# A decoder kernel: its input in three transfers, another form of the Fourier attention's output projection, and ScalarE's lift between its sines

## What is computed

```
scores = einsum('bhqd,bhkd->bhqk', Q, K) / sqrt(D_K) + rel_bias_matrix
x = layernorm(x + softmax(scores) @ V @ Wo.T + bo)
```

```
p  = einsum('blhd,dm->blhm', q or k, proj_mat) / sqrt(D_HEAD)       # m = 128
q', k' = concat([cos(p), sin(p)], -1) / sqrt(D_KMAP)
kv  = einsum('blhm,blhd->bhmd', k', v)
out = einsum('blhm,bhmd->blhd', q', kv).reshape(B, L, 128)
x   = layernorm(x + out @ Wo.T + bo)
```

## Time and profile before

| | |
|---|---|
| median of 3 runs | 1683.41 us (1680.90 to 1689.48) |
| profiled execution, own time | 1688.41 us |
| its span (first to last instruction) | 1686.6 us |
| TensorE busy | 1455.5 us, 86% |
| VectorE busy | 1106.4 us, 66% |
| ScalarE busy | 916.2 us, 54% |
| GpSimd busy | 310.8 us, 18% |
| mean granted clock of TensorE | 0.953 of full speed |
| Fourier phase | from 548.8 to 996.5 us of the span |

### The profile page before, as it was taken

The page is one execution under the profiler, slowest core; times in us unless marked ns, Lnnn a source line. Parts: engine busy times, 40 slices in busy tenths (PEclk is TensorE's granted clock), DMA queues, the critical chain, the costliest instruction groups (busy, mean ns, idle before and its releaser), DMA issues. The chain is left out here.

```text
span 1686.6 us, 31393 instructions
## 1 busy us (share of the span) xinstructions
PE 1455.5 (86%) x12291; PEld 894.3 (53%) x12306; DVE 1106.4 (66%) x2343; ACT 916.2 (54%) x1255; POOL 310.8 (18%) x285
## 2 busy tenths in 40 slices
PE   5999869999798687888888847999999999999972
PEld 3666637777565333433334324566666666666542
DVE  2666646665332598898988952445567667776778
ACT  1332224444454588988888854445565565665433
POOL 2334234443000211101110012111111211210001
PEclk9999979999799799999999986999999999999995
DMA  4000000000000100000000000322222222222220
GB/s 160 2 2 2 2 20 14 12 11 2 1 1 1 51 1 1 1 1 1 1 1 1 1 10 7 71 62 63 68 59 57 69 69 60 60 66 63 57 53 16
DMA packets 39825, 50.73 MB, mean 30 GB/s; under 512 B 9216, under 2 KB 21632, under 8 KB 39296
## 3 DMA queue, kind: packets, MB, share of 16 engines
q1 hardware_dynamic: 39392, 48.06, 11.1%
q10 hardware_dynamic: 288, 0.67, 0.1%
HBM read 13.04 MB, written 2.10 MB: 9 GB/s over the span
## 5 line engine op out<-in xcount | busy, mean ns | idle before, releaser
L1521 DVE TENSOR_TENSOR l_px<-psum,l_share 128x1024 f32<-128x1024 f32 x64 | 78.4, 1225 | 155.5 <-PE psum L1240 101.8
L1381 ACT ACTIVATE l_prob<-psum,l_bias 128x1024 f32<-128x1024 f32 x64 | 71.3, 1114 | 173.6 <-PE psum L1220 173.6
L1229 PE MATMUL psum<-l_XT,l_A 128*128 128x256 f32 x512 | 132.4, 404 | 8.7 <-ACT l_th L1389 6.1
L1215 PE MATMUL psum<-l_th,l_XT 128*128 128x512 f32 x256 | 125.5, 613 | 0.9 <-DVE stream L1528 0.5
L1275 PE MATMUL psum<-l_px,l_N 128*128 128x256 f32 x512 | 124.6, 387 | 1.0 <-ACT l_r L1421 1.0
L1240 PE MATMUL psum<-l_prob,l_X 128*128 128x512 f32 x256 | 123.1, 603 | 0.0
L1229 PEld LDWEIGHTS psum<-l_XT,l_A 128*128 128x128 f32 x512 | 96.9, 200 | 23.0 <-ACT l_th L1389 8.1
L1502 DVE TENSOR_REDUCE l_top<-psum 128x8 bf16<-128x1024 f32 x64 | 78.1, 1221 | 44.8 <-PE psum L1290 44.8
L1275 PEld LDWEIGHTS psum<-l_px,l_N 128*128 128x128 f32 x512 | 94.7, 193 | 18.4 <-issue 4.7
L791 PE MATMUL psum<-f_projX,f_kT 64*128 64x512 f32 x256 | 72.7, 646 | 35.2 <-DVE f_frac L1050 19.2
L793 PE MATMUL psum<-f_qT,f_projX 64*128 64x512 f32 x256 | 72.3, 640 | 32.6 <-DVE f_frac L1050 24.7
(11 more groups left out here) (281 smaller groups left out, 3262.4 us busy)
## 6 DMA issues: line engine op xcount, KB each, us to landing
l_share<-l_recip SPq DMA_DIRECT2D x512, 64.0 KB, 2.0
early_weights<-in_weights SPq DMA_DIRECT2D x1, 2405.0 KB, 15.6
c_cs<-in_ctx SPq DMA_DIRECT2D x16, 128.0 KB, 2.1
f_qf<-in_l_mats SPq DMA_DIRECT2D x1, 2048.0 KB, 7.4
l_craw<-in_ctx SPq DMA_DIRECT2D x16, 128.0 KB, 2.2
out<-l_normed SPq DMA_DIRECT2D x16, 128.0 KB, 2.0
late_weights<-in_weights SPq DMA_DIRECT2D x1, 1089.0 KB, 11.0
relbias<-in_relbias ACTq DMA_DIRECT2D x1, 512.0 KB, 4.6
```

The costliest lines, as they stand in the source:

```text
L1215: nc.tensor.matmul(ps[:, SC + n, :], XT[:, q % 3, k, :, :], th[:, q % 2, k, 8 * n:8 * n + 8, :], start=True, stop=False)
L1229: last = nc.tensor.matmul(ps[:, RO + j // 2, (j % 2) * 256:(j % 2 + 1) * 256], A[:, QB * k + j, :], XT[:, q % 3, :, 1, :], start=True, sto ...
L1381: nc.scalar.activation(prob[:, b % 4, :, :], ps[:, SC:SC + 2, :], ACT.Exp, bias=bias[:, b:b + 1]).then_inc(s["exped"], 1)
L1521: nc.vector.tensor_tensor(px[:, q % 2, :, k, :], ps[:, GA:GA + 2, :].rearrange("p a (h s) -> p (a h) s", s=S), share[:, (b // 2) % 2, b % ...
```

## The change

There are four edits. The input comes in three transfers: 4 tiles, 8 tiles, and the other 20, the last of them with the rest of the weights issued in the first phase (`load_rest`); the bias has a semaphore of its own, and TensorE doesn't wait for VectorE's memsets. At the start of the Fourier phase, VectorE norms the first group and GpSimd does `projX` after that; the waits for `consts` stand later on TensorE and ScalarE. The output projection takes 64 tokens of the kept outputs as stationary operand and the weights as moving one, so that its result has tokens on partitions: copy and transposes are gone, and the residual comes at n = 4 from bank 6. ScalarE's lift stands between sine and cosine of the unit two before.

The diff, cut to its core:

```
@@ attention_phase @@
+        if not cross:
+            @block.sync
+            def _(sp):
+                c["load_rest"](sp)
...
                 if cross:
                     pe.wait_ge(s["staged"], d + 1)
+                elif 2 * d >= FIRST_TILES:
+                    pe.wait_ge(c["x_next"] if 2 * d < FIRST_TILES + NEXT_TILES else c["x_rest"], 16)
...
-            pe.wait_ge(s["v_ones"], 1)
             columns_of(0)
...
                 if not cross:
                     dve.wait_ge(s["scores"], n + 1)
+                    if n == 0:
+                        dve.wait_ge(c["relbias_in"], 16)
@@ fourier_phase, TensorE @@
                 pe.wait_ge(s["o_sb"], g * Q4 + Q4)
-                for batch in range(4):
+                for t in range(T):
                     for q in range(Q4):
-                        at = (batch * Q4 + q) * P
-                        toks = oT[:, q, :].rearrange("p (a b s) -> p a b s", b=4, s=S)[:, :, batch, :]
-                        last = nc.tensor.matmul(ps[:, 6, batch * P:(batch + 1) * P], w("f_wo")[:, at:at + P], toks,
-                                                start=(q == 0), stop=(q == Q4 - 1))
+                        for half in range(2):
+                            at = ((t % 2 * 2 + half) * Q4 + q) * P
+                            toks = slice(t * P + half * S, t * P + half * S + S)
+                            last = nc.tensor.matmul(ps[half * S:half * S + S, 6, t * P:(t + 1) * P], oT[:, q, toks], w("f_wo")[:, at:at + P],
+                                                    start=(q == 0), stop=(q == Q4 - 1))
                 last.then_inc(s["y_ps"], 1)
-            def turn_back(g):
-                pe.wait_ge(s["yT_sb"], g + 1)
-                if g + 1 < G:
-                    pe.wait_ge(s["q_sb"], g + 2)
-                for t in range(T):
-                    last = nc.tensor.transpose(ps[:, 7, t * P:(t + 1) * P], yT[:, t * P:(t + 1) * P], ident)
-                last.then_inc(s["yt_ps"], 1)
-            pe.wait_ge(s["consts"], 6)
             columns_of(0)
             keys_and_values(0)
             queries(0)
+            pe.wait_ge(s["consts"], 6)
             angles(0)
...
-                    if n == 4:
-                        turn_back(g - 1)
@@ fourier_phase, ScalarE @@
             nc.scalar.mul(vb[:, :], w("f_bv"), 1.0 / M).then_inc(s["consts"], 1)
-            act.wait_ge(s["consts"], 6)
...
                 nc.scalar.activation(sin, view(frac[:, N % RING, :]), ACT.Sin, scale=-TWO_PI if n in ON_SCALAR else TWO_PI)
+                if N + 2 < ALL and (n + 2) % UPG in ON_SCALAR:
+                    lift(N + 2)
                 act.wait_ge(s["wrapped"], N + 1)
...
-            def keep_y(g):
...
             columns_of(0)
+            act.wait_ge(s["consts"], 6)
             for N in range(ALL + 5):
                 g, n = divmod(N, UPG)
-                if N + 1 < ALL and (n + 1) % UPG in ON_SCALAR:
-                    lift(N + 1)
...
-                    if n == 3:
-                        keep_y(g - 1)
@@ fourier_phase, VectorE @@
+            for t in range(T):
+                last = nc.vector.tensor_scalar(xs[:, t, :], c["stream"][:, t, :], c["moments"][:, t, 0:1], c["rstd"][:, t:t + 1],
+                                               ALU.subtract, ALU.mult)
+            last.then_inc(s["staged"], 1)
...
-                dve.wait_ge(s["yt_ps"], g + 1)
+                dve.wait_ge(s["y_ps"], g + 1)
                 dve.wait_ge(s["based"], g + 1)
-                nc.vector.tensor_tensor(x, ps[:, 7, :].rearrange("p (t d) -> p t d", d=P), x, ALU.add).then_inc(s["out_read"], 1)
+                nc.vector.tensor_tensor(x, ps[:, 6, :].rearrange("p (t d) -> p t d", d=P), x, ALU.add).then_inc(s["out_read"], 1)
...
-                if g >= 1 and n == 5:
+                if g >= 1 and n == 4:
                     residual(g - 1)
@@ fourier_phase, GpSimd @@
+            pool.wait_ge(s["staged"], 1)
             nc.gpsimd.tensor_tensor(projX[:, :, :], w("f_proj").unsqueeze(1).to_broadcast([P, H, M]),
...
+                if g >= 1:
...
@@ build @@
+        def load_rest(sp):
+            x = ins["x"].rearrange("(n k) s d -> (k s) n d", k=2)
+            sp.dma_start(c["stream"][:, FIRST_TILES + NEXT_TILES:NT, :], x[:, FIRST_TILES + NEXT_TILES:NT, :]).then_inc(c["x_rest"], 16)
+            sp.dma_start(early[:, n_first:n_early], ins["weights"][:, n_first:n_early]).then_inc(loaded_rest, 16)
+            sp.dma_start(late[:, :], ins["weights"][:, n_early:n_w]).then_inc(loaded_rest, 16)
...
             @block.sync
             def _(sp):
+                x = ins["x"].rearrange("(n k) s d -> (k s) n d", k=2)
+                sp.dma_start(c["stream"][:, 0:FIRST_TILES, :], x[:, 0:FIRST_TILES, :]).then_inc(loaded, 16)
                 sp.dma_start(early[:, 0:n_first], ins["weights"][:, 0:n_first]).then_inc(loaded, 16)
-                sp.dma_start(c["stream"][:, :, :], ins["x"].rearrange("(n k) s d -> (k s) n d", k=2)).then_inc(loaded, 16)
...
+                sp.dma_start(c["stream"][:, FIRST_TILES:FIRST_TILES + NEXT_TILES, :],
+                             x[:, FIRST_TILES:FIRST_TILES + NEXT_TILES, :]).then_inc(c["x_next"], 16)
...
-                act.dma_start(c["relbias"][:, :, :], ins["relbias"]).then_inc(loaded, 16)
-                act.wait_ge(loaded, 64)
+                act.dma_start(c["relbias"][:, :, :], ins["relbias"]).then_inc(c["relbias_in"], 16)
+                act.wait_ge(loaded, 48)
```

More of the change, by code:

```diff
@@ L34 @@
 LN_EPS = 1e-5
+FIRST_TILES, NEXT_TILES = 4, 8
 CONST = {"ident": P, "headmask": H, "halfmask": H // 2, "cos": S, "sin": S}
@@ L709, in fourier_phase @@
         "consts lifted staged based xT_ps xT_sb k_ps k_sb v_ps v_sb q_ps q_sb z_ps reduced rounded wrapped feats kv_ps kv_sb kvT_ps kvT_sb o_ps o_sb "
-        "y_ps yT_sb yt_ps steps out_read mats_in ab_ps ab_sb").split()}
+        "y_ps steps out_read mats_in ab_ps ab_sb").split()}
     w, ps = c["w"], c["psum"]
@@ L733, in fourier_phase @@
     kvm = sb("kvm", [P, T // 2, Q4, 2, P])
-    oT, yT = sb("oT", [P, Q4, T * P]), sb("yT", [P, T * P])
+    oT = sb("oT", [P, Q4, T * P])
     half_pi, qb, vb = sb("half_pi", [P, 1]), sb("qb", [P, 1]), sb("vb", [P, P])
@@ L976, in keep_turned @@
                 nc.scalar.copy(kvm[:, pair, :, :, :], ps[:, 6:8, :].rearrange("p a (b e m) -> p (a b) e m", b=2, e=2)).then_inc(s["kvT_sb"], 1)
-            def keep_y(g):
-                act.wait_ge(s["y_ps"], g + 1)
-                nc.scalar.copy(yT[:, :].rearrange("p (a b s) -> p b a s", b=4, s=S),
-                               ps[:, 6, :].rearrange("p (b a s) -> p b a s", b=4, s=S)).then_inc(s["yT_sb"], 1)
             columns_of(0)
+            act.wait_ge(s["consts"], 6)
             for N in range(ALL + 5):
                 g, n = divmod(N, UPG)
-                if N + 1 < ALL and (n + 1) % UPG in ON_SCALAR:
-                    lift(N + 1)
                 if g < G:
@@ L1091, in _ @@
                     pool.wait_ge(s["based"], g)
-                for t in range(T):
-                    tile = g * T + t
-                    last = nc.gpsimd.tensor_scalar(xs[:, t, :], c["stream"][:, tile, :], c["moments"][:, tile, 0:1],
-                                                   c["rstd"][:, tile:tile + 1], ALU.subtract, ALU.mult)
-                last.then_inc(s["staged"], 1)
+                if g >= 1:
+                    for t in range(T):
+                        tile = g * T + t
+                        last = nc.gpsimd.tensor_scalar(xs[:, t, :], c["stream"][:, tile, :], c["moments"][:, tile, 0:1],
+                                                       c["rstd"][:, tile:tile + 1], ALU.subtract, ALU.mult)
+                    last.then_inc(s["staged"], 1)
                 pool.wait_ge(s["staged"], g + 1)
@@ L1795, in build @@
         }
+        def load_rest(sp):
[3 more added lines that the diff above has]
+            sp.dma_start(late[:, :], ins["weights"][:, n_early:n_w]).then_inc(loaded_rest, 16)
+        c["load_rest"] = load_rest
         loaded, loaded_rest = ctx.enter_context(nc.semaphore("loaded")), ctx.enter_context(nc.semaphore("loaded_rest"))
+        for n in ("x_next", "x_rest", "relbias_in"):
+            c[n] = ctx.enter_context(nc.semaphore(n))
         early_room = ExitStack()
@@ L1802, in _ @@
             def _(sp):
+                x = ins["x"].rearrange("(n k) s d -> (k s) n d", k=2)
+                sp.dma_start(c["stream"][:, 0:FIRST_TILES, :], x[:, 0:FIRST_TILES, :]).then_inc(loaded, 16)
                 sp.dma_start(early[:, 0:n_first], ins["weights"][:, 0:n_first]).then_inc(loaded, 16)
-                sp.dma_start(c["stream"][:, :, :], ins["x"].rearrange("(n k) s d -> (k s) n d", k=2)).then_inc(loaded, 16)
-                sp.dma_start(early[:, n_first:n_early], ins["weights"][:, n_first:n_early]).then_inc(loaded_rest, 16)
-                sp.dma_start(late[:, :], ins["weights"][:, n_early:n_w]).then_inc(loaded_rest, 16)
```

(2 more changed lines are left out.)

## The result

| | before | after |
|---|---|---|
| median of 4 runs each, us | 1685.22 (1680.9 to 1689.48) | 1665.5 (1663.96 to 1667.58) |
| ratio, 95% interval | | 0.9884 [0.9864, 0.9904] |
| profiled execution: own time, span, us | 1688.41, 1686.6 | 1663.96, 1662.1 |

The changed kernel is faster by 19.7 us between the medians, by 24.5 between the two profiled spans. Forecast were 1662 us, 21.4 less; the range 1652 to 1672 holds the 1665.5.

The account below looks back on a forecast made before the run. Barrier-separated phases wait at their starts; in the Fourier periods no engine is full and VectorE's waits set the pace. 8.9 + 5.7 + 1.2 + 5.6 = 21.4 us off the 1683.41 median gives 1662; range 1652 to 1672.

Parts of the forecast that it names:

- Start of the program: First barrier needs less input and TensorE skips the memset wait: first transpose at 6.5 us, 8.9 us earlier (7.6 to 9.7).
- the sum over four transfers: Program start: 1.29 MB in four transfers, 2.2 + 3.2, lands at 5.4 us; upper bound 6.7 with all five.
- Start of the Fourier phase: VectorE norms the first group, GpSimd does `projX` behind it: transposes 5.7 us earlier (4.5 to 5.8), `projX` covered by 0.4.
- Projection: Output projection as 32 matmuls on alternating array halves: 3.9 us a block, +0.1 a group (bounds 3.8 to 7.5).
- rival of 1692 us: Projection halves run one after another: 7.5 us a block, 30 us over eight groups, slower than before; chance 0.04.
- Tail: Last Fourier group: the copy and transposes back, bare there, go; 1.34 us less 0.1 gives 1.2 us.
- Period: Fourier groups, keys to keys: 0.7 + 0.2 - 0.1 = 0.8 us a group, seven groups, 5.6 us.
- ScalarE's stretch: ScalarE from the lift of unit 5 to the copy, 25.10 us before: a gain of 0.7 us a group.
- the lift frees VectorE wholly: Fourier groups: lifts out of the way gain 2 us a group rather than 0.8, 1654 us; fewer or freed VectorE 0.12.
- Only the starts pay: Rival: ScalarE's cosine behind the lift eats what the earlier residual frees in the groups; 1668 us, chance 0.12.
- The clock: TensorE's granted clock in the Fourier periods: three falls to 1.2 GHz kept; none to seven falls, -4.9 to +6.6 us.
- rival of more falls: Seven falls of TensorE's clock in the Fourier periods: 1662 + 6.6 = 1669 us; chance 0.06.

Follow-up runs that it names:

- e9: e8 with `relbias` and the second part of `x` issued on SP behind the first barrier: 1648.34 us, ratio to before 0.9771.
- e8: Changed kernel with the lift of unit 5 behind the cosine of unit 3, plus three unused matmuls twice a group: 1648.78 us, ratio 0.9785.
- e5: Kernel before plus three unused 256-column matmuls twice a group from group 1 on, ahead of angles 0 and 2: 1684.15 us, ratio 0.9989.
- e12: Changed kernel with TensorE's wait for VectorE's memsets put back in the cross attention: 1672.12 us, a single execution.
- e11: e7 with the projection's four matmuls of each array half in a row instead of alternating: 1667.85 us, one execution, not read for its total.
- e7: Changed kernel plus three unused 256-column matmuls twice a group from group 1 on: 1654.67 us, ratio to before 0.9821.
- e10: e7 with ScalarE's lift back in its old place, ahead of the sine of the unit before: 1654.62 us, ratio to before 0.9805.
- e6: Changed kernel with old projection, residual and lift place (starts alone), plus three unused matmuls twice a group: 1669.96 us, ratio to before 0.9907.

## Why the prediction was right, and where its terms were off

**Start of the program, predicted 8.9: right as a mechanism, 0.8 too much at the transpose.** The weights landed at 6.6, not at 5.4. The step that failed is the sum over four transfers: with the second part of `x` the upper bound of 6.7 was the value to take. The transfers beside the weights hold them up: e9 takes two of them away, and the weights land 4.1 us after their issue instead of 5.0 (e8) or 5.4. From the landing it took 0.7 us rather than 1.1. The whole phase is shorter by 9.6 between the profiled spans, about 9 if the mean of e5 and before (210.82, 212.42) is set against that of the kernels with the new start (201.3 to 204.5). The last microsecond beyond 8.1 was not traced.

**Start of the Fourier phase, predicted 5.7: 5.8 measured.** The cover over `projX` was 0.3 us where 0.4 was worked out. It held in every kernel with the new start.

**Cross attention: not in the sum, 1.6 us (e12).** `columns_of(0)` is one function for two phases. The dropped wait was followed in the first one only.

**Projection, predicted 3.9 us: 3.71.** The halves overlap, as their single records show (7 ns apart). The Trainium skill (TensorE: Matmul & The Clock Gate, Part 3) lets a weight load overlap a running matmul only when its row group differs, and by that the 64 loads of a block would lie bare. The trace disagrees: weight loads and matmuls of a block have 3.47 and 3.71 us of busy time within the same 3.71, and even with the halves one after another it is 4.54. The rival of 1692 us decided from 2.7 us extra a group. The block is shorter than before instead, and even e11's has only 0.83 more than e7's: it is refuted.

**Tail, predicted 1.2: 1.45 measured.** It is 5.21 less 3.76: 1.34 for the copy and the transposes back, as read in the prediction, and 0.11 for the block, which was forecast 0.1 longer and came 0.1 shorter.

**Period, predicted 0.8: 1.36 without a fall.** By the steps of the prediction: up to the lift of unit 5, +0.1 predicted, -0.11 measured (from the keys 23.37 us after and 23.48 before, in the period that begins at 716.00 and has no fall), which is the shorter block. ScalarE's stretch, -0.7 predicted, 24.18 - 25.10 = -0.92 measured. From the copy to the keys, -0.2 predicted, 3.21 - 3.53 = -0.32 measured. The last two had the right sign and were too small; the first had the wrong sign, but is a tenth of a microsecond. That it is ScalarE's chain is shown by e8 (one cosine out of the stretch: 50.67 to 49.82, -0.85 of its 1.04) and e11 (0.83 more on TensorE ahead of the lift: 0.83 more a period). The rival "the lift frees VectorE wholly" is refuted by e10: in the changed kernel the lift's place makes the period 0.5 us longer, since it puts a cosine behind a lift that waits; the gain is that of the projection and the earlier residual, which no run takes apart. "Only the starts pay" is refuted by the periods: 52.03 us in e6, which has only the starts, and 50.67 in e7.

**The clock, predicted three falls as before: seven.** From the second keys to the end of the phase the prediction had 6.8 us (5.6 and 1.2). Without falls six periods of 1.36 give 8.2, and from the last keys on it is 2.6 (68.80 before, 66.17 in e7, the same kernel with no fall that costs anything), together 10.8. Seen were 4.9: the six periods 5.4 (317.63 to 312.26), the rest -0.5 (68.80 to 69.32). The difference of 5.9 is the four more falls, two of them in the periods (2.8) and two behind the last keys (3.1). The sum came out near by luck, in that errors of both signs met: 1.6 of the cross attention and 4.0 more from the new code against 5.9 for the clock. The rival of more falls, given 0.06, named the number that came, seven; the time, 1665.5, lies midway between the forecast's 1662 and its 1669 only since the rest of the change gave more. It deserved a larger share.

**What stays open.** Where falls come is not predicted by anything seen here. The same idle time of 2.1 us had a fall behind it at 648 and none at 700. Filling two gaps removed the seven in e7 and only moved the three in e5. Nor is it settled why the last phase, with unchanged code, takes 685 to 694 us. And 1.5 of the 3.1 us of the cross attention, 0.8 of the last phase and 0.5 of the Fourier phase's first period (50.29 us before, 49.84 after) are in the 24.5 us between the spans, but in no term.

## What to carry to other kernels

When a wait goes that several phases share, follow it in each of them. Sum a stage along the engine that has no idle time left behind the point where it starts, and ask of an instruction that is moved ahead of another whether it waits for something: the lift that waited 2.9 us held up a cosine that was ready (e8). Price the gaps of TensorE with the clock in mind: here the same change was worth 19.7 us with the gaps as they were and 29.5 with two of them filled in both kernels (e5 to e7).

## What the runs showed of the hardware

- A few unused matmuls made the kernel faster: 1.56 us of them twice a group from the second group on, 10.8 us in all (e7), since TensorE's granted clock no longer fell to 1.2 GHz in the periods. In the kernel before, the same matmuls gave nothing that could be told (e5).
- An `outputs` block of 16 matmuls took 1.93 us at the upper level of the clock and 3.34 to 3.52 where it fell.
- f32 matmuls with 64 stationary and 128 moving columns, on the two halves of the array in turn: 3.71 us for 32, so 0.116 each; with each half's four in a row: 4.54, 0.142 each. With 128 stationary columns it was 0.236.
- 385 KB took 3.8 us to land as the first transfer of its queue with three more issued behind and beside it, 5.0 to 5.7 behind a first one of 256 KB with three more under way, and 4.1 behind the same one with only the constants beside them (e9).
